# 64-query transposes for one attention key block, and one shift product for both row tiles

## What is computed

```python
def shift_token(t):                      # second half of the channels comes from the token before
    t1, t2 = jnp.split(t, 2, axis=-1)
    t2 = jnp.pad(t2, ((0, 0), (1, 0), (0, 0)))[:, :-1]
    return jnp.concatenate([t1, t2], axis=-1)

qkv = shift_token(x) @ wqkv              # 8 heads of 64
q, k = rotary_xpos(l2norm(q) * qs, l2norm(k) * ksc)
sim = q @ k.T                            # windows of 64 keys: a query sees its own window up to
mask = (i < j) | (i > j + 64)            # itself, and the window before, from its own place on
o = softmax(sim) @ v
x = x + o @ wo
h = layernorm(shift_token(x)) * lg + lb
a, g = jnp.split(h @ w1 + b1, 2, axis=-1)
x = x + (a * gelu(g)) @ w2 + b2
```

## Time and profile before

| | us |
|---|---|
| median of 3 runs (lowest, highest) | 2874.21 (2873.69, 2874.41) |
| the profiled execution, its own time | 2875.4 |
| its span, first to last instruction | 2873.6 |
| TensorE busy | 2647.1 |
| VectorE busy | 2260.1 |
| ScalarE busy | 2225.5 |
| GpSimd busy | 1223.4 |

### The profile page before, as it was taken

One profiled execution on the slowest core, in us unless ns is written; L12 is line 12 of the kernel. 1 busy time (PEld: TensorE's weight loads), 2 busy tenths in 40 slices (PEclk: granted clock), 3 DMA queues, 4 the chain that ended last, 5 costly groups with the idle time before them and its releaser, 6 DMA issues. The chain is left out here.

```text
span 2873.6 us, 55943 instructions
## 1 busy us (share of the span) xinstructions
PE 2647.1 (92%) x18868; PEld 1819.6 (63%) x18868; DVE 2260.1 (79%) x3798; ACT 2225.5 (77%) x6114; POOL 1223.4 (43%) x1089
## 2 busy tenths in 40 slices
PE   6888888789999999999999999997899999999997
PEld 3454445356666666666777777774566666666665
DVE  8999999976767777777689999996667777676774
ACT  5788878557777777777799999995677777777775
POOL 5776777664444444444400000001444444444442
PEclk8999999999999999999999999997999999999998
DMA  3000000000000000000000000000000000000000
GB/s 98 1 1 1 1 1 1 0 1 2 1 1 1 13 13 1 1 1 1 13 14 2 2 2 1 2 1 1 1 2 1 1 2 13 17 5 7 7 7 7
DMA packets 15672, 17.84 MB, mean 6 GB/s; under 512 B 3838, under 2 KB 12863, under 8 KB 15295
## 3 DMA queue, kind: packets, MB, share of 16 engines
q1 hardware_dynamic: 15390, 14.26, 1.7%
HBM read 12.16 MB, written 2.10 MB: 5 GB/s over the span
## 5 line engine op out<-in xcount | busy, mean ns | idle before, releaser
L1064 POOL TENSOR_TENSOR f_p<-f_p,f_rs 128x512 f32<-128x512 f32 (+1 forms) x256 | 321.2, 1255 | 907.4 <-DVE f_rs L1013 907.3
L901 ACT ACTIVATE f_p<-pair,f_nm 128x128 f32<-128x128 f32 (+1 forms) x1024 | 387.4, 392 | 125.2 <-DVE f_nm L1002 125.2
L679 POOL TENSOR_TENSOR m_hc<-m_h,m_c 128x512 f32<-128x512 f32 x256 | 323.4, 1284 | 154.5 <-DVE m_h L646 120.5
L1056 POOL TENSOR_TENSOR f_qb<-f_kn,f_tab 128x512 f32<-128x512 f32 x256 | 373.5, 1480 | 24.3 <-DVE f_kn L981 21.0
L646 DVE TENSOR_TENSOR_SCAN m_h<-m_a,pair 128x1024 f32<-128x1024 f32 x128 | 292.2, 2283 | 11.6 <-ACT m_a L608 1.9
L767 PE MATMUL pair<-f_wqkv,f_hT 128*128 128x512 f32 x512 | 248.7, 609 | 18.0 <-DVE f_kn L981 14.5
L608 ACT ACTIVATE m_a<-m_delta,m_A 128x255 f32<-128x255 f32 x512 | 217.3, 496 | 59.4 <-DVE m_h L646 58.8
L533 PE MATMUL bank<-m_hc,ident 128*128 128x512 f32 x512 | 248.2, 619 | 1.4 <-DVE X L655 1.3
L815 PE MATMUL pair<-ident,f_p 128*128 128x128 f32 x1536 | 244.7, 282 | 3.7 <-DVE f_pT L1007 2.4
L855 PE MATMUL bank<-f_hnT,f_w 128*128 128x256 f32 (+1 forms) x768 | 213.4, 401 | 12.5 <-ACT f_g L933 3.1
L815 PEld LDWEIGHTS pair<-ident,f_p 128*128 128x128 f32 x1536 | 170.6, 141 | 82.2 <-issue 60.0
(11 more groups left out here) (181 smaller groups left out, 6159.2 us busy)
## 6 DMA issues: line engine op xcount, KB each, us to landing
f_wqkv<-in_f_wqkv SPq DMA_DIRECT2D x4, 768.0 KB, 4.0
out_x<-X SPq DMA_DIRECT2D x16, 128.0 KB, 1.8
f_w<-in_f_w SPq DMA_DIRECT2D x4, 341.0 KB, 3.3
f_wo<-in_f_wo SPq DMA_DIRECT2D x4, 256.0 KB, 2.7
sel<-in_sel SPq DMA_DIRECT2D x1, 768.0 KB
f_w<-in_f_w SPq DMA_DIRECT2D x4, 192.0 KB, 3.2
m_taps<-in_m_taps SPq DMA_DIRECT2D x1, 512.0 KB, 3.6
X<-in_x SPq DMA_DIRECT2D x1, 512.0 KB, 8.5
```

What stands on the lines that cost most here:

```text
L679: op = nc.gpsimd.tensor_tensor(m_hc[:, g % 4, n], m_h[:, g % 2, n], m_c[:, g % 2, n].unsqueeze(1).broadcast_to([P, EC, L]), ALU.mult)
L901: op = nc.scalar.activation(f_p[:, t, j, k0:k1], SC[:, j, k0:k1], ACT.Exp, bias=f_nm[:, t, j:j + 1], accum_out=f_sm[:, t, j:j + 1])
L1056: op = nc.gpsimd.tensor_tensor(f_qb[:, t, :, o].rearrange("p (x h) d -> p x h d", x=2), f_kn[:, t, :, 32 - 32 * e:64 - 32 * e].rearrange(" ...
L1064: op = nc.gpsimd.tensor_tensor(f_p[:, t, :, k0:k1], f_p[:, t, :, k0:k1], f_rs[:, t, :].unsqueeze(2).broadcast_to([P, 4, k1 - k0]), ALU.mult)
```

## The change

For t = 1, y = 0 the four transposes take only the first 64 queries: the weight block is f_p with 64 partitions by 128 keys, the stream is a 64 by 64 identity, and the four results lie side by side, 64 columns each, in the first half of PT_PS. ScalarE's copy reads them there, as many elements as before. The second edit writes the shift of both tiles as one product with 128 columns, followed by the carry into the second half. Everything else, the lists of steps and all waits included, is as it was.

```diff
@@ f_pe, step pT @@
                     pe.wait_ge(*dve_f.at(i - back, f"pe{part}1"))
+                n = W if t and not y else P
                 for j in range(4):
-                    mm = nc.tensor.transpose(PT_PS[:, j * P:j * P + P], f_p[:, t, j, y * P:y * P + P], ident[:])
+                    mm = nc.tensor.transpose(PT_PS[:, j * n:j * n + n], f_p[0:n, t, j, y * P:y * P + P], ident[0:n, 0:n])
@@ f_pe, step sh @@
                 zt = tiles(f_z1[:])
-                nc.tensor.matmul(bank[1][:, 0:64], shift[:], zt[:, 0, 64:128], start=True, stop=True)
-                nc.tensor.matmul(bank[1][:, 64:128], shift[:], zt[:, 1, 64:128], start=True, stop=False)
-                mm = nc.tensor.matmul(bank[1][:, 64:128], carry[:], zt[:, 0, 64:128], start=False, stop=True)
+                nc.tensor.matmul(bank[1][:, 0:128], shift[:], zt[:, :, 64:128], start=True, stop=False, skip_group_check=True)
+                mm = nc.tensor.matmul(bank[1][:, 64:128], carry[:], zt[:, 0, 64:128], start=False, stop=True,
+                                      skip_group_check=True)
@@ f_act, step pe @@
                     op = nc.scalar.activation(f_pT0[:, g, :, P:P + W],
-                                              PT_PS.rearrange("p (c k) -> p c k", c=4)[:, :, 0:W], ACT.Copy)
+                                              PT_PS[:, 0:4 * W].rearrange("p (c k) -> p c k", c=4), ACT.Copy)
```

## The result

| | before | changed kernel |
|---|---|---|
| median of 5 runs (lowest, highest), us | 2874.28 (2873.69, 2874.43) | 2858.6 (2854.93, 2861.58) |
| ratio (95% interval) | | 0.9943 (0.993 to 0.9957) |
| the profiled execution, us | 2875.4 | 2854.93 |

The change makes the kernel 15.7 us faster, 0.6%; forecast were 18.1 and a time of 2856.1. The five runs of the changed kernel lie within 6.7 us of each other, those of before within 0.8 (but 21 later runs of before, beside e5 to e7, spread over 4.5: 2871.90 to 2876.44); what the profiles show of that scatter stands under `after_again`. In the changed kernel the lines from L814 on are one higher.

What follows compares the result with a forecast made beforehand. Bound: TensorE's list, with excursions from the shift over hb to hn and through the gelu. 63 x 0.22 = 13.9 (shift) plus 60 x 0.07 = 4.2 (pT110) make 18.1 us less, 2874.2 to 2856.1; range 2847 to 2867.

Steps and rivals of the forecast that it cites:

- What bounds the kernel: Steady loop of phase f: mostly TensorE's list, turn 26.14 us, with excursions from the shift over hb to hn and through gelu.
- The shift: In front of f_hb: two of six passes removed, 0.63 to 0.41, so 0.22 us less a turn, passing whole to hnT.
- 0.11 a pass: In the shift: the ordinary load of 128 columns decides, so each pass costs 0.11 us though 64-column streams need half.
- pT110: Four transposes between L829 and xT: save 0.22, xT pays 0.15 for going back to full array; 0.07 us less a turn.
- pT100: Transposes between v1 and hnT: pay 2 x 0.15, save 0.22; the +0.08 is covered by TensorE's wait for hn.
- The clock: Its tail was left out of the range; half-clock stretches inside the loops were named as what would make the forecast wrong.
- The sum: Whole kernel: 13.9 for the shift plus 4.2 for pT110, together 18.1 us less, median 2856.1.
- The slot stays at 0.11: Rival at pT110: the load decides, costing 0.10 more a turn; 7.9 us less in all, 2866.3; 20%.
- No half array: Rival at pT110 and xT: 64 rows no half array, or going back free; 27.1 us less, 2847.1 at best; 12%.
- Each transpose drains: Rival at pT110: 0.15 paid before each of the four, +0.38 a turn; 8.9 us slower in all, 2883.1; 4%.
- The gain is taken back: Rival: an unseen wait between hb and hnT, or together with the first rival; under 5.7 us change, about 2870; 7%.

Runs made afterwards that it cites:

- e5: Kernel before, still with three shift products, the first widened to stream 128 columns: 2872.14 us, ratio 0.9997.
- e7: Changed kernel with the shift moved ahead of qk1 in TensorE's list: 2874.22 us, ratio 1.0003.
- after_again: The changed kernel run once more, unaltered, for the scatter of its runs: 2860.55 us, ratio 0.9954.
- e1: Kernel before with the shift's edit only: 2859.16 us, ratio 0.9947.
- e2: Kernel before with the 64-query transposes only (pT100 and pT110): 2873.92 us, ratio 0.9995.
- e4: Changed kernel with pT100 back at 128 queries, so only pT110 is narrow: 2859.08 us, ratio 0.9941.
- e6: Changed kernel with pT110 moved in TensorE's list behind the scores s00, which also have 64 rows: 2895.79 us, ratio 1.0076.
- e3: Changed kernel with pT110 back at 128 queries, so only pT100 is narrow: 2859.89 us, ratio 0.9948.
- e9: Changed kernel with pT000 and shift ahead of qk1 on TensorE and pT000's copy before hb on ScalarE; hn not moved: 2860.03 us, ratio 0.9953.
- e8: Changed kernel with pT000 and shift ahead of qk1, pT000's copy before hb, and hn ahead of ss1 on VectorE: 2918.6 us, ratio 1.0159.
- e10: e8 with hn computed by VectorE's operation with two tensor operands instead of two per-partition scalars: 2926.15 us, ratio 1.0182.

## Why the prediction was right

**What bounds the kernel.** That the path passes through the shift, hb and hn was right. e1 moved the turn by 0.22 us, where the shift's pieces lost 0.23; in the changed kernel the 63 waits of ScalarE for the shift fell by 0.23 on average.

**The shift.** Forecast 0.63 -> 0.41; measured 0.40. The reason given, that the load of 128 columns sets the pace and a stream of the same width is free, is shown by e5, whose loads follow each other every 0.11. The prediction's "0.11 a pass" holds for such a row of passes, not for each: its own 0.17 for L843 is one pass of 0.11 and one of 0.06.

**pT110.** Forecast: 0.37 for the four, 0.37 for xT, 0.07 less a turn. Measured: 0.39, 0.37, and 0.05 less (e2, e4). The mechanism held in both halves: xT pays 0.15 for going back to the full array, and nothing is paid between two 64-row forms (e6). The term was a little mis-sized: a slot of 64 columns is (0.39 - 0.15) / 4 = 0.06, not 0.055; in 60 turns 3.0 us instead of 4.2. A term of this size could only be read from the turn.

**pT100.** Counted as nothing in the sum; e3 and e4 show just that. But the reason has the sign wrong: the prediction let pT100 pay 2 x 0.15, save 0.22 and so eat 0.08 of TensorE's wait for hn, and the wait grew, by 0.16 a turn (13.4 us in all over the waits of load and product). The way back to the full array has no price that shows behind a wait: hnT holds 0.44 before and after. Nothing hung on this term here; where TensorE doesn't wait it would have been read wrongly.

**The clock.** The sum has no term for it. The stretches at half clock moved the time by 5.1 us in one profile of the changed kernel, and by nothing in the other. Of before, show one of 6.7 us at a clock of 0.50; behind it come four, of together 37.6 us, of which 20.5 were missing in the profile after. The 20.5 were worth about 5.

**The sum.** 18.1 forecast, 15.7 measured, 16.0 in the loops of the profiled executions. Of the difference 1.2 is pT110's slot. What is left, about 1 us, is less than the scatter between two sets of runs of the changed kernel (2858.6 and 2860.55).

**The rivals.** "The slot stays at 0.11" would have shown 0.59 at pT110; it was 0.39. These transposes follow each other at 0.06, though they load 128 columns, the ordinary loads of the shift at 0.11. "No half array" would have left xT at 0.22; it was 0.37. "Each transpose drains" would have shown 0.8; it was 0.39. "The gain is taken back" had something in it, as e7 and e9 show: other ways stand so close behind (over pT000 and p01 in e7, over s01 in e9) that a shift which is only moved gives nothing. It did not happen in the change, most likely since the shift stands ahead of them all in TensorE's list.

## What to carry to other kernels

Price a small product by the time until the next can start, which the chain shows, not by its record: in fp32 with 128 weight columns a row of passes goes on at 0.11 us a pass even where the streams are narrower (six took 0.63, four 0.40), so join products with the same weights; and add 0.15 us for each change between half and full array before cutting one, unless a wait stands behind it. Shortening a step that stands ahead of both branches of a fork paid in full here; moving it earlier helped one branch, and the other, or a wait for the step's own input, took over. Where a gain is below what the runs can tell, compare the steady turn of the loop in the chain, which here repeats to 0.01 or 0.02 us at the same place of the loop.

## What the runs showed of the hardware

- A weight load of a transpose is quicker than one of an ordinary fp32 product of the same 128 columns: 139 to 142 ns as recorded, for 64 and for 128 rows alike, against 191. With streams of 64 columns such transposes follow each other at 0.06 us (four hold 0.25 in e6), while ordinary loads of the shift follow each other at 0.11 under streams of 64 and of 128 columns (e5).
- Four 64-row transposes hold 0.25 us behind 64-row products (e6), 0.39 behind L830 with 64 weight columns (e2), and full-array work right behind them pays 0.15 for the way back (xT, 0.37 in place of 0.22): only a change of form is priced.
- VectorE's hn (128x128 in fp32), where it starts beside GpSimd's multiply of f_qb, ended only when that had ended: 1075 ns in e8 and 1140 in e10 for one, in place of about 340, so in both of the forms that were run. The reduction nm01 in the same place took its ordinary 0.69 us in both runs.
- The mean granted clock of one and the same stretch of 607 to 612 us came out as 0.97 or 0.99 in different executions, worth 5 us. That is a third of what the change gives, and has nothing to do with it: the changed kernel shows both. In e8 the clock was at half at eight places inside the loops, 3.4 us each, where the changed kernel has 1.00 (613.6 to 1402, 2033 to 2831).
